# A small FFN with a long convolution in front: K sums straight from the powers, another order ahead of tile 0 and in tiles 1 and 2, and the last tile in two halves

## The chip, the cores and the metric

One NeuronCore of a Trainium2 chip runs the kernel. The metric is the time of one execution on the device in microseconds; three runs of the kernel before gave 215.28, 215.71 and 215.75 us, the median is 215.71.

## What is computed

`x` has 64 sequences, 32 heads and 512 positions. Per head, a kernel K of 512 values is a sum over 64 complex powers, K(h, l) = 2 Re sum_n Cs(h, n) exp(dtA(h, n) l); x, masked by a length per sequence, is convolved with it, and `D` times x is added. On each row of 512 values comes a feed-forward net with quantised operands:

```
beta = mean(|x|);  xq = clip(round(x * sqrt7 / (beta + eps)), -8, 7) * beta
w_eff = clip(round(w / (mean|w| + eps)), -1, 1) * mean|w| * scale      # each of w_gate, w_up, w_down
gate = xq @ w_gate.T;  up = xq @ w_up.T                                # 512 -> 1376
inter = up * square(relu(gate));  inter is rounded to 8 bits by its row's maximum
out = x + inter @ w_down.T                                             # 1376 -> 512
```

## The kernel before, in words

The 2048 rows are worked on in T = 16 tiles of 128 rows (two heads of 64 sequences each). Each engine has its own list of instructions, written out by hand; semaphores join them. What each engine does stands in its own block: SP issues most DMAs, `pool` (GpSimd) some, `pe` is TensorE, `act` ScalarE, `dve` VectorE.

**Ahead of tile 0.** VectorE computes the powers `f` of each head by doubling (`double`, L910) in two tables, 1 to 31 and the multiples of 32, and multiplies the second by `cs`. K is then a sum over the 64 powers, real and imaginary, for each pair (coarse step, fine step): one matmul with 128 rows, 16 columns of weights and 32 moving columns per head. For it VectorE copies the operands of one half of the heads (`g`) to all 128 partitions (`table_b` L936, `table_a` L942). `k_head` (L533) is the matmul; there are 4 heads in part 0, and 12 and 16 in parts 1 and 2 (`K_PARTS` L281). An f32 matmul is two instructions in the trace. `k_copy` (L988) adds D and turns the order, and SP (part 0) and GpSimd's queue (parts 1, 2; L440) store K to DRAM, from where `load_toep` (L328) reads it as a Toeplitz matrix for a tile. SP waits for the store of both last parts before it loads x and the Toeplitz tile of tile 2 (L344, `load_ahead` L347).

Meanwhile each weight matrix is loaded in parts. ScalarE sums its absolute values (`weight_sum` L638); a matmul with a constant takes the mean over the partitions (`mean` L455); VectorE takes the inverse (`weight_mean` L917); `weight_round` rounds to integers (L645 on ScalarE, L955 on VectorE); TensorE turns blocks of it (`turn_inner` L505, groups 0 to 5 for the gate weights, 6 to 11 for the up weights, four PSUM banks in turn), and `weight_copy` clips what was turned, on ScalarE (blocks 2, 4, 5, 9, 11) or VectorE (the others). The down weights are rounded (VectorE L958, ScalarE L649), turned by DMA (`turn_down` L355, on SP) and clipped by `down_copy` (L961) on VectorE. `keep_clock` (L521) is filler: matmuls whose result nobody reads.

**A tile.** `xt` (L467) turns x on TensorE, `xt_copy` on ScalarE takes it out of PSUM, `conv` (L474) is the convolution, `y_mask` (L968, VectorE) masks it, `y_sum` (L662, ScalarE) sums, `y_scale` (L974, VectorE) makes the scales, `y_round` (L667, ScalarE) rounds, `qt` (L486) turns the result and `q_copy` (L983, VectorE) clips it. `products` (L557) are four gate and four up matmuls for each of three blocks of columns (416, 512, 448). `relu_square` (L700) on ScalarE and `gated` (L1040) on VectorE make `inter`. VectorE takes the row's maximum, quantises `inter` to `inter_q` (L1103), SP turns that by DMA (L367), VectorE casts it to `i_t` (L1073), `down` (L594) is the down product of eleven matmuls, and L1121 scales it and adds x; SP stores it (L373). In iteration k TensorE runs the products of tile k, the down product of tile k-1, the q turn of tile k+1 and the convolution of tile k+2; in iteration 1 the down product stands last.

**The last tile.** Its `inter_q` is made in two cuts (L1110) and turned by TensorE instead of DMA (`turn_last` L575, behind eight filler matmuls). ScalarE casts the first six blocks (L719), VectorE the other five (L1080, L1082).

```
            for h in range(HG):
                k_head(2, h)
                if h >= K_EARLY:
                    mm = k_head(1, h)
```

## Time and profile before

| | us |
|---|---|
| median of three runs | 215.71 |
| the profiled execution | 215.85 |
| its span | 214.1 |
| TensorE busy in the span | 180.8 |
| VectorE busy | 168.0 |
| ScalarE busy | 115.0 |

The span is the time from the first to the last event of the profiled execution. A busy time counts the time in which an instruction of the engine ran; matmuls overlap, so that TensorE's is the union. The granted clock is a share of 2.4 GHz: 1.00 is that, 0.50 is 1.2 GHz. In a timeline the brackets say how long the engine was idle before the group, and what released it.

### The profile page before, as it was taken

Reading aid. Unit: us, or ns where it says so; the run is one execution under the profiler, and the core shown is the slowest. Engines: PE = TensorE matmul, PEld = TensorE weight load, DVE = VectorE, ACT = ScalarE, POOL = GpSimd, SP = SyncE. Lnnn points to the kernel's source line nnn. Section 1 sums busy time; section 2 is a strip of 40 time slices with the busy share of each in tenths; the row PEclk is TensorE's granted clock in tenths of the full one; section 3 lists DMA queues with packets and bytes.
Section 4 is the critical chain, followed back from the end, with each engine's and each line's share of the span. In section 5 each row is a group of like instructions: output and inputs, shape, how many; then the busy total and the mean of one; then the engine's idle time right before and its main releaser. Section 6 shows DMA issues by size and latency. Waiting matters only on the chain.

```text
span 214.1 us, 3425 instructions
## 1 busy us (share of the span) xinstructions
PE 180.8 (84%) x1136; PEld 97.0 (45%) x1136; DVE 168.0 (78%) x457; ACT 115.0 (54%) x184; POOL 11.0 (5%) x29
## 2 busy tenths in 40 slices
PE   1011679499969999999999999999999999998882
PEld 1011576345524554545454545454545545454340
DVE  5999886579987979696968787786969696969841
ACT  2277949829943645545463728282736455464410
POOL 4034502000000000000000000000000000000000
PEclk9999999969999999999999999999999999999999
DMA  3999849426999676667483949484757667070722
GB/s 79 370 385 307 283 122 336 140 74 170 168 202 227 189 162 195 146 169 175 139 213 118 221 116 225 114 243 91 227 116 203 126 190 150 15 164 5 165 49 49
DMA packets 43488, 36.61 MB, mean 171 GB/s; under 512 B 29872, under 2 KB 29952, under 8 KB 43472
## 3 DMA queue, kind: packets, MB, share of 16 engines
q1 hardware_dynamic: 42816, 34.93, 62.6%
q10 hardware_dynamic: 336, 1.41, 1.9%
q0 software_dynamic: 320, 0.06, 0.3%
q8 instruction: 9, 0.15, 0.3%
q14 instruction: 7, 0.06, 0.1%
HBM read 25.27 MB, written 4.28 MB: 138 GB/s over the span
## 4 chain that ended last, share of the span: by engine, by line
PE 71%; DVE 11%; ACT 8%; issue 3%; DMA 3%; SPq 2%; DVEq 0%
PE down_ps L607 18%; PE gate_ps L566 16%; PE up_ps L571 15%; PE conv_ps L481 15%; PE tr_act_ps L471 2%; DMA int_gate<-int_down 2%; ACT int_up L642 2%; PE tr_dve_ps L494 1%; ACT int_gate L649 1%; ACT int_down L642 1%; ACT int_up L649 1%; DVE inter L1046 1%; PE tr_dve_ps L536 1%; DMA c_in<-in_L_cond_C_dram 1%; SPq L358 1%
## 5 line engine op out<-in xcount | busy, mean ns | idle before, releaser
L705 ACT ACTIVATE g<-gate_ps,gu_scale 128x416 f32<-128x416 f32 (+2 forms) x48 | 30.5, 636 | 66.5 <-issue 55.6
L1046 DVE SCALAR_TENSOR_TENSOR inter<-up_ps,gu_scale,g 128x416 f32<-128x416 f32 (+2 forms) x48 | 33.1, 690 | 18.3 <-ACT g L708 18.2
L566 PE MATMUL gate_ps<-gate_t,q_t 128*128 128x416 bf16 (+2 forms) x192 | 45.2, 358 | 1.1 <-DVE q_t L985 1.1
L571 PE MATMUL up_ps<-up_t,q_t 128*128 128x416 bf16 (+2 forms) x192 | 45.5, 360 | 0.0
L607 PE MATMUL down_ps<-down_t,i_t 128*128 128x512 bf16 (+1 forms) x176 | 40.7, 380 | 2.2 <-DVE i_t L1073 1.0
L481 PE MATMUL conv_ps<-toep,x_t 128*64 128x512 f32 (+3 forms) x256 | 39.1, 449 | 0.1
L1050 DVE TENSOR_REDUCE imax<-inter 128x1 f32<-128x416 f32 (+2 forms) x48 | 30.3, 631 | 1.6
L708 ACT ACTIVATE g<-g 128x416 f32<-128x416 f32 (+2 forms) x48 | 28.1, 586 | 1.5
L571 PEld LDWEIGHTS up_ps<-up_t,q_t 128*128 128x128 bf16 x192 | 18.8, 98 | 18.5 <-issue 0.2
L607 PEld LDWEIGHTS down_ps<-down_t,i_t 128*128 128x128 bf16 (+1 forms) x176 | 17.0, 98 | 22.4 <-DVE i_t L1073 1.4
L481 PEld LDWEIGHTS conv_ps<-toep,x_t 128*64 128x64 f32 x256 | 17.2, 139 | 20.7 <-issue 16.8
L566 PEld LDWEIGHTS gate_ps<-gate_t,q_t 128*128 128x128 bf16 x192 | 17.6, 98 | 16.1 <-issue 2.2
L971 DVE SCALAR_TENSOR_TENSOR y<-steps,lens,conv_ps 128x512 f32<-128x512 f32 x16 | 12.0, 747 | 5.5 <-PE conv_ps L481 5.3
L1103 DVE TENSOR_SCALAR inter_q<-inter,iscale 128x1376 int16<-128x1376 f32 x15 | 14.0, 937 | 0.5
L1121 DVE SCALAR_TENSOR_TENSOR o_sb<-down_ps,oscale,x_res 128x512 f32<-128x512 f32 x16 | 11.9, 744 | 2.8 <-PE down_ps L607 2.8
L669 ACT ACTIVATE y_r<-y,round_col,yscale 128x512 f32<-128x512 f32 x16 | 12.8, 801 | 0.3 <-DVE yscale L981 0.3
L665 ACT ACTIVATE y_r<-y 128x512 f32<-128x512 f32 x16 | 9.9, 616 | 4.5 <-DVE y L971 4.5
L463 PE MATMUL down_ps<-wsum,averaging 128*128 128x1 f32 x14 | 3.1, 327 | 10.6 <-ACT int_gate L642 10.2
L471 PE MATMUL tr_act_ps<-ident,x_in 128*128 128x128 f32 x64 | 9.9, 278 | 0.0
L471 PEld LDWEIGHTS tr_act_ps<-ident,x_in 128*128 128x128 f32 x64 | 8.1, 146 | 2.9 <-issue 0.2
L660 ACT COPY x_t<-tr_act_ps 128x512 f32<-128x512 f32 x16 | 9.1, 567 | 0.0
L642 ACT ACTIVATE int_gate<-raw_gate 128x3072 bf16<-128x3072 f32 (+1 forms) x2 | 5.1, 2550 | 6.6 <-DMA raw_gate<-in_L_ffn_w_gate_dram 6.6
(170 smaller groups left out, 165.4 us busy)
## 6 DMA issues: line engine op xcount, KB each, us to landing
toep<-k_back SPq DMA_DIRECT2D x16, 512.0 KB, 5.1
x_in<-in_x_dram SPq DMA_DIRECT2D x32, 128.0 KB, 2.8
x_res<-in_x_dram SPq DMA_DIRECT2D x32, 128.0 KB, 4.0
out_dram<-o_sb SPq DMA_DIRECT2D x32, 128.0 KB, 2.5
raw_gate<-in_L_ffn_w_gate_dram SPq DMA_DIRECT2D x1, 1536.0 KB, 7.2
raw_up<-in_L_ffn_w_up_dram SPq DMA_DIRECT2D x1, 1536.0 KB, 13.9
raw_down<-in_L_ffn_w_down_dram ACTq DMA_DIRECT2D x1, 1376.0 KB, 6.9
raw_down<-in_L_ffn_w_down_dram SPq DMA_DIRECT2D x1, 1376.0 KB, 9.0
```

The source lines that it names most:

```text
L471: mm = pe.transpose(tr_act_ps[:, i * P:(i + 1) * P], x_in[p][:, i * P:(i + 1) * P], ident[:])
L481: mm = pe.matmul(conv_ps[half * B:(half + 1) * B, 0:L - i * P], x_t[:, i, half * B:(half + 1) * B], toep[p][:, half, i * P:L], start=(i == ...
L566: mm = pe.matmul(gate_ps[bank][:, 0:cn], q_t[p][:, i, :], gate_t[:, i, c0:c0 + cn], start=(i == 0), stop=(i == KB - 1))
L571: mm = pe.matmul(up_ps[bank][:, 0:cn], q_t[p][:, i, :], up_t[:, i, c0:c0 + cn], start=(i == 0), stop=(i == KB - 1))
L607: mm = pe.matmul(down_ps[:], i_t[0:r, c, :], down_t[0:r, c, :], start=(c == 0), stop=(c == IB - 1))
L669: nc.scalar.activation(y_r[:], y[:], ACT.Identity, bias=round_col[:], scale=yscale[:]).then_inc(y_rounded, 1)
L705: nc.scalar.activation(g2[bank][:, 0:cn], gate_ps[bank][:, 0:cn], ACT.Relu, scale=gu_scale[p][:, 0:1]).then_inc(relu_done, 1)
L708: nc.scalar.activation(g2[bank][:, 0:cn], g2[bank][:, 0:cn], ACT.Square).then_inc(g2_ready, 1)
L971: v.scalar_tensor_tensor(out=y[:], in0=steps[:], scalar=lens[:], in1=conv_ps[:, ::-1], op0=ALU.is_lt, op1=ALU.mult).then_inc(y_masked, 1)
L1046: v.scalar_tensor_tensor(out=inter[:, c0:c0 + cn], in0=up_ps[bank][:, 0:cn], scalar=gu_scale[p][:, 1:2], in1=g2[bank][:, 0:cn], op0=ALU.mu ...
L1050: return v.tensor_reduce(imax[:, c:c + 1], inter[:, c0:c0 + cn], AX.X, ALU.max, apply_absolute_value=True)
L1103: v.tensor_scalar(inter_q[:, 0:I], inter[:], iscale[:], None, ALU.mult).then_inc(inter_quant, 1)
```

## The change

`mean` is one matmul (two instructions) whose columns, one for each part of the sums, VectorE adds up; the mean of the gate weights is read between the products and the sums of the doubling from 4. The K sums take their operands from `f` and from a single table `ka` on the partitions where they stand: for each head two matmuls of 64 rows, real and imaginary, that accumulate. The order of the parts is changed (the second half of the heads comes before the rest of the first), and TensorE's order ahead of tile 0 is: part 0, mean of the up weights, x turn of tile 0, turns 3 to 8, part 1, convolution of tile 0, x turn of tile 1, turns 9 to 11, part 2, q turn. VectorE's and ScalarE's orders follow. The down product of tile 0 moves from the end of iteration 1 into iteration 2, and its output with it; ScalarE rounds y of tile 2 before the last relu and square of tile 1; VectorE copies the second half of the down weights after the quantising of tile 1. Of the last tile, ScalarE quantises the last five blocks and casts them, VectorE the first six; the down product runs as two halves of 256 columns in two PSUM banks, each scaled, added and stored by itself, the last store on two queues; two filler matmuls are left of eight, and the two ahead of tile 0's convolution are gone.

```diff
         f = sb("f", [P, 2, 2 * HG, JB + 1])
-        ka = [sb(f"ka{g}", [P, HG, JA]) for g in range(2)]
-        kb = [sb(f"kb{g}", [P, HG, JB]) for g in range(2)]
+        ka = sb("ka", [P, 2, HG, JA])
...
         K_EARLY = 4
-        K_PARTS = [(0, 0, K_EARLY), (0, K_EARLY, HG), (1, 0, HG)]
+        K_PARTS = [(0, 0, K_EARLY), (1, 0, HG), (0, K_EARLY, HG)]
+        LAST = [(conv_ps, slice(0, L // 2)), (up_ps[0], slice(L // 2, L))]
...
                     turn_down(0)
-                if k >= 2:
+                if k == T + 1:
+                    sp.wait_ge(out_ready, T)
+                    for half in range(2):
+                        sp.dma_start(in_dram(out, T - 1, half)[:, LAST[0][1]],
+                                     o_sb[p][half_rows(half), LAST[0][1]]).then_inc(stored[p], 16)
+                    sp.wait_ge(out_ready, T + 1)
+                    sp.dma_start(in_dram(out, T - 1, 0)[:, LAST[1][1]],
+                                 o_sb[p][half_rows(0), LAST[1][1]]).then_inc(stored[p], 16)
+                elif k >= 2:
...
                 n = len(ARRIVE[m]) - 1
-                for i in range(n):
-                    mm = pe.matmul(down_ps[:, m:m + 1], averaging[:], wsum[:, m, i:i + 1],
-                                   start=(i == 0), stop=(i == n - 1))
+                mm = pe.matmul(down_ps[:, 4 * m:4 * m + n], averaging[:], wsum[:, m, 0:n], start=True, stop=True)
...
-            def k_head(i, h):
-                g = K_PARTS[i][0]
-                dst = tr_dve_ps[32 * i:32 * i + JA, h * JB:(h + 1) * JB]
-                return pe.matmul(dst, ka[g][:, h], kb[g][:, h], start=True, stop=True)
-            for h in range(K_EARLY):
-                mm = k_head(0, h)
-            mm.then_inc(k_summed, 1)
+            def k_sums(i):
+                g, h0, h1 = K_PARTS[i]
+                rows_g = slice(g * N, (g + 1) * N)
+                for h in range(h0, h1):
+                    for c in range(2):
+                        mm = pe.matmul(tr_dve_ps[32 * i:32 * i + JA, h * JB:(h + 1) * JB], ka[rows_g, c, h],
+                                       f[rows_g, c, h, 0:JB], start=(c == 0), stop=(c == 1))
+                mm.then_inc(k_summed, 1)
+            k_sums(0)
             mean(1)
-            pe.wait_ge(tables_ready, 2)
-            for h in range(HG):
-                k_head(2, h)
-                if h >= K_EARLY:
-                    mm = k_head(1, h)
-            mm.then_inc(k_summed, 1)
+            xt(0, 0, 0)
             turn_inner(0, 0, range(3, IG))
-            xt(0, 0, 0)
             turn_inner(1, IG, range(0, 3))
-            keep_clock(2)
+            k_sums(1)
...
             turn_inner(1, IG, range(3, IG))
+            k_sums(2)
...
             def turn_last():
                 pe.wait_ge(y_masked, T)
-                keep_clock(8)
+                keep_clock(2)
...
             def down(m, k):
                 if k == T:
-                    pe.wait_ge(it_act_copied, 1)
-                else:
-                    pe.wait_ge(it_dve_copied, m)
+                    pe.wait_ge(it_dve_copied, T)
+                    for bank, cols in LAST:
+                        for c in range(IB):
+                            if c == IT_SPLIT:
+                                pe.wait_ge(it_act_copied, 1)
+                            r = P if c < IB - 1 else IR
+                            mm = pe.matmul(bank[:, 0:L // 2], i_t[0:r, c, :], down_t[0:r, c, cols],
+                                           start=(c == 0), stop=(c == IB - 1))
+                        mm.then_inc(down_done, 1)
+                    return
+                pe.wait_ge(it_dve_copied, m)
...
                 for c in range(IB):
-                    if c == IT_SPLIT and k == T:
-                        pe.wait_ge(it_dve_copied, m)
...
                     products(m, p, 1, k)
+                    if k == 2:
+                        down(1, 1)
...
                     conv(m + 2, j + 1, p)
-                if k == 1:
-                    down(m, k)
...
             weight_copy(2)
+            xt_copy(0)
...
             weight_copy(5)
-            xt_copy(0)
...
                 if k == T:
-                    act.wait_ge(it_turned, 1)
+                    act.wait_ge(iscale_ready, 1)
+                    act.wait_ge(it_loaded, 16 * (T - 1))
+                    cut = slice(IT_SPLIT * P, I)
+                    nc.scalar.activation(inter_q[:, cut], inter[:, cut], ACT.Copy,
+                                         scale=iscale[:]).then_inc(inter_quant, 1)
+                    act.wait_ge(it_turned, 2)
                     act.wait_ge(down_done, T - 1)
-                    nc.scalar.copy(i_t[:, 0:IT_SPLIT, :].rearrange("p c t -> p (c t)"),
-                                   tr_act_ps[:, 0:IT_SPLIT * P // 2].bitcast(I16)).then_inc(it_act_copied, 1)
+                    nb = IB - 1 - IT_SPLIT
+                    nc.scalar.copy(i_t[:, IT_SPLIT:IB - 1, :].rearrange("p c t -> p (c t)"),
+                                   tr_dve_ps[:, 0:nb * P // 2].bitcast(I16))
+                    nc.scalar.copy(i_t[0:IR, IB - 1, :], tr_dve_ps[0:IR, nb * P // 2:(nb + 1) * P // 2].bitcast(I16)
+                                   ).then_inc(it_act_copied, 1)
+                    act.wait_ge(out_ready, T + 1)
+                    act.dma_start(in_dram(out, T - 1, 1)[:, LAST[1][1]],
+                                  o_sb[1][half_rows(1), LAST[1][1]]).then_inc(stored[1], 16)
...
                     y_round(1)
+                if k == 1:
+                    y_round(2)
...
                     relu_square(2)
-                if 1 <= k < T - 1:
+                if 2 <= k < T - 1:
...
-            def double(k, n, heads):
+            def double(k, n, heads, between=None):
...
                              [f[:, c:c + 1, 0:heads, k:k + 1] for c in range(2)])
+                if between:
+                    between()
...
             def weight_mean(m, step):
                 dve.wait_ge(w_mean_ps, m + 1)
-                v.tensor_copy(wscale[:, m:m + 1], down_ps[:, m:m + 1])
-                step(v.tensor_scalar(weps[:, m:m + 1], down_ps[:, m:m + 1], EPS, None, ALU.add))
+                step(v.tensor_reduce(wscale[:, m:m + 1], down_ps[:, 4 * m:4 * m + len(ARRIVE[m]) - 1], AX.X, ALU.add))
+                step(v.tensor_scalar(weps[:, m:m + 1], wscale[:, m:m + 1], EPS, None, ALU.add))
...
             while k < JB:
-                double(k, k, 2 * HG if k < JA else HG)
+                double(k, k, 2 * HG if k < JA else HG, (lambda: weight_mean(0, step)) if k == 4 else None)
                 k *= 2
-                if k == 8:
-                    weight_mean(0, step)
...
             def k_copy(i):
                 g, h0, h1 = K_PARTS[i]
-                dve.wait_ge(k_summed, min(i, 1) + 1)
+                dve.wait_ge(k_summed, i + 1)
...
-            table_b(0)
-            table_a(0)
-            table_b(1)
+            v.tensor_tensor(ka[:, 0, :, ::-1], by_csr[:, 0], by_csi[:, 1], ALU.subtract)
+            v.scalar_tensor_tensor(out=ka[:, 1, :, ::-1], in0=by_csi[:, 0], scalar=-1.0, in1=by_csr[:, 1],
+                                   op0=ALU.mult, op1=ALU.subtract).then_inc(tables_ready, 1)
+            weight_copy(0)
...
             k_copy(0)
+            weight_copy(1)
             weight_mean(1, step)
-            table_a(1)
-            weight_copy(0)
-            weight_copy(1)
...
             weight_copy(7)
-            k_copy(1)
-            k_copy(2)
+            weight_copy(8)
...
             step(v.tensor_tensor(wscale[:, 0:2], wscale[:, 0:2], scl[:, 0:2], ALU.mult))
-            weight_copy(8)
+            k_copy(1)
             y_mask(0)
+            weight_copy(10)
             y_scale(0, 0, step)
-            weight_copy(10)
+            k_copy(2)
...
+                def add_out(n, bank, cols, done):
+                    q = n % 2
+                    dve.wait_ge(down_done, done)
+                    dve.wait_ge(res_loaded[q], 32 * (n // 2 + 1))
+                    wait(dve, stored[q], 32 * (n // 2))
+                    v.scalar_tensor_tensor(out=o_sb[q][:, cols], in0=bank[:, 0:cols.stop - cols.start],
+                                           scalar=oscale[q][:], in1=x_res[q][:, cols],
+                                           op0=ALU.mult, op1=ALU.add).then_inc(out_ready, 1)
...
                     down_copy(1)
-                if k == 1 or k == T - 1:
+                if k == 2:
+                    y_scale(3, 1, step)
+                if k in (1, 2, T - 1):
                     gated(1)
+                if k == 2:
+                    add_out(0, down_ps, slice(0, L), 1)
...
                     v.tensor_copy(i_t[:], it_int[:]).then_inc(it_dve_copied, 1)
-                if 2 <= k < T - 1:
+                if 3 <= k < T - 1:
...
                 if k == T:
-                    dve.wait_ge(it_turned, 2)
+                    dve.wait_ge(it_turned, 1)
                     dve.wait_ge(down_done, T - 1)
...
+                    v.tensor_copy(i_t[:, 0:IT_SPLIT, :].rearrange("p c t -> p (c t)"),
+                                  tr_act_ps[:, 0:IT_SPLIT * P // 2].bitcast(I16)).then_inc(it_dve_copied, 1)
+                    add_out(T - 2, down_ps, slice(0, L), T - 1)
+                    for h, (bank, cols) in enumerate(LAST):
+                        add_out(T - 1, bank, cols, T + h)
-                if k < T - 1 and k != 1:
+                    v.tensor_copy(i_t[:, 0:IT_SPLIT, :].rearrange("p c t -> p (c t)"),
+                                  tr_act_ps[:, 0:IT_SPLIT * P // 2].bitcast(I16)).then_inc(it_dve_copied, 1)
+                    add_out(T - 2, down_ps, slice(0, L), T - 1)
+                    for h, (bank, cols) in enumerate(LAST):
+                        add_out(T - 1, bank, cols, T + h)
+                if k < T - 1 and k not in (1, 2):
...
                     step(gated(2))
-                if k == 1:
-                    down_copy(0)
...
                     step(v.tensor_scalar(gam127[:], gamma[:], EPS, 1.0 / 127.0, ALU.add, ALU.mult))
-                    step(v.reciprocal(iscale[:], gam127[:]))
                     if k != T - 1:
+                        step(v.reciprocal(iscale[:], gam127[:]))
...
+                        v.reciprocal(iscale[:], gam127[:]).then_inc(iscale_ready, 1)
+                        dve.wait_ge(iscale_ready, 1)
                         dve.wait_ge(it_loaded, 16 * (T - 1))
-                        for cut, ready in ((slice(0, IT_SPLIT * P), last_quant), (slice(IT_SPLIT * P, I), inter_quant)):
-                            v.tensor_scalar(inter_q[:, cut], inter[:, cut], iscale[:], None,
-                                            ALU.mult).then_inc(ready, 1)
+                        cut = slice(0, IT_SPLIT * P)
+                        v.tensor_scalar(inter_q[:, cut], inter[:, cut], iscale[:], None,
+                                        ALU.mult).then_inc(last_quant, 1)
                 if k == 1:
+                    down_copy(0)
                     y_mask(3)
-                if k is None or k >= 1:
...
+                if 2 <= k < T - 1:
+                    add_out(m - 1, down_ps, slice(0, L), m)
```

## Rows read from the trace of the kernel before

**Rows 1.** Page, section 1: busy time and share of the span of each engine.

```profile
PE 180.8 (84%) x1136; PEld 97.0 (45%) x1136; DVE 168.0 (78%) x457; ACT 115.0 (54%) x184; POOL 11.0 (5%) x29
```

**Rows 2.** Chain that ended last, start us, us, work: first gate products of two tiles.

```profile
97.17 0.81 PE gate_ps L566 x4
...
107.27 0.81 PE gate_ps L566 x4
```

**Rows 3.** Timeline (start us, us, engine, line, operation): the mean and rounding of gate weights.

```profile
15.11 1.01 PE L463 MATMUL down_ps<-wsum,averaging 128*128 128x1 f32 x4 [10.24 <-ACT int_gate L642]
...
16.14 0.44 DVE L907 TENSOR_TENSOR inter<-f 128x256 f32<-128x256 f32 x1
...
17.60 2.86 ACT L649 ACTIVATE int_gate<-raw_gate,winv 128x3072 int16<-128x3072 f32 x1 [2.55 <-DVE winv L922]
```

**Rows 4.** Timeline, 24 to 38 us: K sums, turns, first copy behind them, convolution.

```profile
24.83 0.60 PE L536 MATMUL tr_dve_ps<-kb,ka 128*16 128x32 f32 x8 [1.51 <-DVE ka L946]
...
28.60 1.89 PE L536 MATMUL tr_dve_ps<-kb,ka 128*16 128x32 f32 x56 [1.40 <-DVE ka L946]
...
31.25 1.38 PE L517 MATMUL up_ps<-ident_bf,int_gate 128*128 128x128 bf16 x12
...
32.35 1.41 ACT L656 ACTIVATE gate_t<-up_ps 128x1024 bf16<-128x1024 int16 x2 [3.41 <-PE up_ps L517]
...
33.11 1.06 PE L517 MATMUL gate_ps<-ident_bf,int_up 128*128 128x128 bf16 x16
...
34.98 2.37 PE L481 MATMUL conv_ps<-toep,x_t 128*64 128x512 f32 x16
```

**Rows 5.** Timeline, 41 to 48 us: tile 0's start and tile 1's convolution.

```profile
41.30 0.40 PE L494 MATMUL tr_act_ps<-ident_bf,y_r 128*128 128x128 bf16 x4 [2.30 <-ACT y_r L669]
...
42.08 3.01 DVE L1024 TENSOR_REDUCE wsum<-raw_down 128x1 f32<-128x2752 f32 x1
...
42.22 0.88 PE L566 MATMUL gate_ps<-gate_t,q_t 128*128 128x416 bf16 x4 [0.52 <-DVE q_t L985]
...
44.25 3.50 PE L481 MATMUL conv_ps<-toep,x_t 128*64 128x512 f32 x16
...
47.80 0.75 DVE L971 SCALAR_TENSOR_TENSOR y<-steps,lens,conv_ps 128x512 f32<-128x512 f32 x1 [1.53 <-PE conv_ps L481]
```

**Rows 6.** Window of that convolution: us, TensorE busy, granted clock, DMA share, GB/s.

```profile
44.20:47.80 3.60, 3.60 (x18) 0.67 0.04 13
```

**Rows 7.** Timeline, 61 to 67 us, TensorE at the end of tile 1.

```profile
61.04 0.40 PE L494 MATMUL tr_dve_ps<-ident_bf,y_r 128*128 128x128 bf16 x4 [1.28 <-ACT y_r L669]
61.50 2.37 PE L481 MATMUL conv_ps<-toep,x_t 128*64 128x512 f32 x16
64.45 2.54 PE L607 MATMUL down_ps<-down_t,i_t 128*128 128x512 bf16 x11 [0.58 <-DVE down_t L966]
```

**Rows 8.** Timeline, from 204 us: filler matmuls, cast, last down product, output, stores.

```profile
204.20 1.89 PE L525 MATMUL conv_ps<-steps,ident_bf 128*128 128x512 bf16 x8
...
206.47 0.80 ACT L719 CAST i_t<-tr_act_ps 128x768 bf16<-128x768 int16 x1 [5.13 <-PE tr_act_ps L582]
...
207.32 2.55 PE L607 MATMUL down_ps<-down_t,i_t 128*128 128x512 bf16 x11 [0.61 <-ACT i_t L719]
209.91 0.75 DVE L1121 SCALAR_TENSOR_TENSOR o_sb<-down_ps,oscale,x_res 128x512 f32<-128x512 f32 x1 [2.61 <-PE down_ps L607]
...
210.69 1.11 SPq L373 DMA_DIRECT2D out_dram<-o_sb  x2
```

**Rows 9.** DMA issues: KB each, median us from issue to landing.

```profile
toep<-k_back SPq DMA_DIRECT2D x16, 512.0 KB, 5.1
...
k_back<-k_sb POOLq DMA_DIRECT2D x1, 24.0 KB, 2.9
```

**Rows 10.** Groups by shape, K sums: busy us, mean ns of one.

```profile
L536 PE MATMUL tr_dve_ps<-kb,ka 128*16 128x32 f32 x64 | 2.5, 240 | 2.9 <-DVE ka L946 2.9
...
L536 PEld LDWEIGHTS tr_dve_ps<-kb,ka 128*16 128x16 f32 x64 | 2.2, 121 | 3.3 <-DVE ka L946 3.3
```

24 lines of the change are left out of this document (2 added, 22 removed).

## The prediction

> **What bounds the kernel now.** I read the busy shares first [rows 1]: TensorE is busy for 84% of the span, VectorE for 78%, ScalarE for 54%. That average mixes three stages, so I then read the chain of work that ended last, in order of time. From 66.8 us to about 195 us it is TensorE alone: each tile's first gate product starts 10.10 us after the last one's [rows 2] and nothing waits. The change leaves these tiles alone, so what it can win lies ahead of tile 3 and behind tile 15, and whatever TensorE gains before tile 3 is carried unchanged to the tail. The rest I read from timelines, engine by engine.
>
> Ahead of tile 0 the chain goes: sums of the weights on ScalarE, the mean on TensorE and VectorE, the rounding on ScalarE, the K sums and the turns on TensorE, then ScalarE's queue (two weight copies, the x copy, a rounding and a sum over weights, the sum of y), which had waited 3.41 us for the turns behind the K sums [rows 4]. Behind it, tile 0's products start at 42.22, and the convolution of tile 1 takes 3.50 us where that of tile 0 took 2.37 [rows 4, 5]; the granted clock of that stretch is 0.67 [rows 6]. In tile 1 TensorE waits 1.28 us before the q turn and 0.58 us before the down product [rows 7]. At the end it is one serial chain: quantise, turn, cast, down product, scale and add, store [rows 8].
>
> **The sum is made against the profiled execution**: 215.85 us, with a span of 214.1; the 1.75 us around the span I leave as they are. It is 0.14 us over the median of the runs shown, which I take off at the end.
>
> **Part 1, the means.** The mean of the gate weights was four instructions in 1.01 us and becomes two, some 0.5 us (15.11 to 15.6). VectorE now reads it between the products and the sums of a doubling, that is behind the product that ends at 16.14 + 0.44 = 16.58 [rows 3]. Three dependent steps of about 0.2 us give the inverse at 17.2; the rounding on ScalarE then starts at 17.23 where it was 17.60: 0.37 us earlier. ScalarE's queue is unbroken from there to the rounding of the rest of the gate weights, which ends at 27.66 (28.03 before). The mean of the up weights, six such instructions, becomes two as well, 0.5 us; its result comes at about 25.7 and no longer ends a wait.
>
> **Part 2, tables and K sums.** Four copies of 0.42 us on VectorE go, and the table of both halves is two operations of the same 0.42 us each, on 128 partitions where it was 64 (I take the same time, since the number of elements per partition is the same). The first K sums can start at 24.05 instead of 24.83. The price: 64 matmul instructions become 128. Before, the run of 56 took 1.89 us, 30 ns apart behind a latency of 0.24; the first 8 took 0.60 us, 51 ns apart [rows 4]. No 64-row matmul is in the trace. With half the rows it might take half, 15 ns: the low bound (on the path it would give back 64 x 15 ns = 1.0 us). 51 ns is the high one, and I take 30, since 56 instructions are the better sample and the number of columns stays. So: 0.8 us for the first part, 2.1 for the second (64), 1.6 for the third (48). The first part, its copy and its store on SP all come 0.7 us earlier, and with them the loads of the first two Toeplitz tiles.
>
> **Part 3, the order ahead of tile 0.** TensorE: the x turn runs in the idle time before 27.7. Then 20 turns from 27.7 and 24 more. Here is a clock effect: the turns from 31.25 run about 0.107 us apart (12 in 1.38 less a latency of some 0.2), those from 33.11 about 0.056 apart (16 in 1.06) [rows 4], so by these durations TensorE went from 1.2 to 2.4 GHz near 32.5, after 4 us of unbroken work (the granted clock is written as 1.00 on both sides). I put the rise at about 32. The turns then end at 32.2, the second K sums at 34.2, and the convolution of tile 0 starts there instead of at 34.98 (the two filler matmuls are gone; its Toeplitz tile was issued at 28.71 and is now issued at 28.0, which with the page's 5.1 us is 33.1). It ends at 36.55, and VectorE masks y at 36.6. ScalarE is no longer late: copies to 31.0, rounding to 33.4, sum to 35.9, so it waits for y and sums it by 38.1. But weight copy 10 now stands ahead of the scale of y on VectorE, and it waits for a turn behind the convolution: it runs from 37.9 to 38.6. The scale is ready at 39.25, y rounded at 40.1, q turned at 40.55 (the third K sums end at 39.9 and are just covered), q copied at 41.0 behind the K copy, and the products start at 41.07. Against 42.22 that is 1.15 us.
>
> **Part 4, the clock.** Before, TensorE had idled 2.30 us before the q turn, and 0.52 us after it [rows 5], and the clock then fell to 1.2 GHz. Now the K sums fill that hole and 0.3 and 0.5 us remain. I take it that the clock holds: tile 0's first products take 1.57 us instead of 2.03 and the convolution 2.37 instead of 3.50, together 1.6 us. The next link is VectorE: its sum over the down weights (3.01 us) and the first gated block (some 1.25 us) end at 45.15, and only then can it mask y of tile 1, where it was 47.80 [rows 5]. So 2.65 of 2.75 us are kept.
>
> **Part 5, what was moved behind.** The third K copy ends at 40.55 where it was 36.35; its store on GpSimd's queue lands 2.9 us after its issue [rows 9], and SP's loads of x and the Toeplitz tile for tile 2 stand behind it: x issued at 43.4, the tile at 44.6, landed by 47 and, with 5.1 us, by 49.7. TensorE wants them at 47.2 and 49.5. I count nothing for this, since the queues are nearly empty by then, with 0.7 us as the high bound.
>
> **Part 6, the first down product.** It moves from behind tile 1 into tile 2, behind the second products. The wait of 0.58 us before it (it waited for the copy of the transposed down weights, [rows 7]) goes. The 1.28 us before the q turn stays in another form: the convolution of tile 3 needs the x copy on ScalarE, which is behind the same work whether the rounding of y comes before or after the last relu and square. VectorE's order in tile 2 becomes down copy, mask, block 0, scale, block 1, output of tile 0, cast of tile 1: in the new times the cast ends at 68.1 and TensorE wants it at 68.7. So 0.5 us of cover; I take a loss of 0.1. Products of tile 3: 2.65 + 0.58 - 0.1 = 3.1 us earlier. In tile 2 SP's next x and Toeplitz loads stand behind the later output of tile 0 (67.75 against 67.78), which is some 4 us ahead of their use.
>
> **Part 7, the tail** (in the old times). Six of eight filler matmuls go (1.89 us for eight, less a latency of 0.17): 6 x 0.215 = 1.3 us, so the first turns end at 205.2 instead of 206.45; the second turns wait for ScalarE's share of the quantising (608 columns at 0.86 ns, from the rounding of 3072 in 2.86, [rows 3]: 0.75 us from 203.75), done by 204.5, and end at 205.5. VectorE casts six blocks in about 0.6 us, and the down product starts at 205.83 against 207.32. Its halves of 256 columns take 11 x 0.11 each and end at 207.2 and 208.4; ScalarE's casts are done at 206.35, just ahead of the sixth block. The output of tile 14 lies between, covered. The last half is scaled and added in 0.5 us (0.75 for 512 columns, [rows 8]), ready at 208.95 instead of 210.66. The last stores are issued from two queues, at 209.0, where the second of the pair was issued at 211.2. Gain 2.2 us; 1.5 if the small stores or casts cost as much as the large, 2.7 if the waits vanish.
>
> **Sum:** 215.85 - 3.1 - 2.2 = 210.55, less 0.14: **210.4 us**.
>
> **The rivals.**
> The clock falls again, 0.17. For it: the new work in the hole is turns and 32-column matmuls, and two short holes stay. Against it: just such work, K sums and turns from 28.60 to 32.4, raised the clock [rows 4]. It costs up to 1.6 us: **212.0**.
>
> The Trainium skill, "TensorE: Matmul & The Clock Gate", Part 4 on the transpose mode, says that transposes don't count as busy for the clock; by that rule this rival would be the likely one, but the rise at 32 us in this trace speaks against it.
>
> K sums at 51 ns, 0.12. The second part costs 1.3 us more and delays the convolution; the third costs 1.0 more and is no longer covered before the q turn. The start of tile 0 is then 43.2, the clock holds: **212.5**.
>
> The ends ahead of tile 0 don't move, 0.07: weight copy 10, the third K copy and late loads eat what the order gave, and the clock falls. Then only 0.5 and 2.2 us are left: **213.0**.
>
> Slower, 0.05. Weight load and matmul of the 64-row form are not overlapped. A load takes 121 ns and a matmul 240 ns by itself [rows 10]; at 121 ns each, the 112 instructions of the last two parts cost 112 x 0.09 = 10.2 us more, some **220.6**. It turns slower from 80 ns each (5.3 / 112 = 47 ns over my 30). Against it: 128-row K sums, with the same 16 columns loaded, ran 30 ns apart. The Trainium skill, "TensorEngine Tiling (Array Packing)", Key Properties, says that a change of the tiling mode drains TensorE. Here the mode would change twice for each part, six times in all, and not for each matmul; no row shows such a drain.
>
> The forecast itself has 0.59.
>
> **How the numbers follow.** The likeliest is the forecast, 210.4. Its own range is 209.2 to 211.5: 0.5 and 0.7 us for the tail, 0.7 for the prologue's end and the loads. The range of 8 in 10 takes in the two rivals at 212.0 and 212.5: 209.0 to 212.7. A measurement of this kernel can tell about 0.2% (0.4 us) from no change. All cases but the slower one lie over 2 us below 215.71. Of the 0.07 of the fourth case I give 0.02 to the same time, should the tail's gain not come either. That leaves 0.93 for faster, 0.02 for the same, 0.05 for slower.
>
> **What would show it.** Right: the q turn of tile 0 with under 0.6 us of idle time before it, the convolution of tile 1 in 2.4 us at a granted clock of 1.00, K sums of 64 instructions in about 2.1 us, no wait before the first down product, a last down product in two groups, begun 6.1 us before the end of the span. Wrong: K sums over 3 us, a clock of 0.5 in the first tile, TensorE waiting for x or the Toeplitz tile of tile 2, or for a cast in tile 2.

## The result, and the profile after

The changed kernel took 212.11 us in the median of four runs (211.16 to 212.98), the kernel before 215.5 (213.64 to 215.75); the ratio is 0.986, with a 95% interval of 0.982 to 0.990. The profiled execution took 211.90 us, with a span of 210.0, against 215.85 and 214.1: 3.95 us less. The forecast was 210.4. The direction was right, and the time lies in the range of 8 in 10 (209.0 to 212.7), but above the forecast's own range (209.2 to 211.5); in the profiled execution the gain is 1.35 us smaller than forecast.

One thing of the runs has to be known. The kernel before doesn't take one time: of 43 runs, 20 took 215.2 to 215.9 us (the long runs) and 23 took 213.4 to 214.6. All those seen ahead of the prediction were of the first group. What makes the difference is not shown; what the traces say of it stands with the experiments on the tail and on the hole.

The page of the changed kernel: busy shares, and the granted clock in tenths (9 is 0.9 or more), in 40 slices of 5.25 us.

```profile
PE 178.1 (85%) x1179; PEld 98.2 (47%) x1195; DVE 165.4 (79%) x450; ACT 115.8 (55%) x186; POOL 10.6 (5%) x29
...
PEclk9999958999999999999999999999999999999999
```

The busy share hardly moved [rows 1]; the clock dips in the sixth and seventh slice, 26 to 37 us, and nowhere else; the steady tiles still follow each other every 10.10 us. The gain is at both ends. TensorE ahead of tile 0, and below it VectorE's mask, weight copy 10 and mask of tile 1, in the timeline of the changed kernel; [rows 3 to 5] are the same places before:

```profile
23.75 0.64 PE L546 MATMUL tr_dve_ps<-f,ka 64*16 64x32 f32 x16 [1.06 <-DVE ka L1008]
...
28.28 1.38 PE L525 MATMUL up_ps<-ident_bf,int_gate 128*128 128x128 bf16 x12
...
32.15 2.47 PE L546 MATMUL tr_dve_ps<-f,ka 64*16 64x32 f32 x64
34.54 2.38 PE L489 MATMUL conv_ps<-toep,x_t 128*64 128x512 f32 x16
...
38.50 1.58 PE L546 MATMUL tr_dve_ps<-f,ka 64*16 64x32 f32 x48
40.67 0.40 PE L502 MATMUL tr_act_ps<-ident_bf,y_r 128*128 128x128 bf16 x4 [0.59 <-ACT y_r L680]
41.59 0.88 PE L571 MATMUL gate_ps<-gate_t,q_t 128*128 128x416 bf16 x4 [0.52 <-DVE q_t L995]
...
43.10 2.37 PE L489 MATMUL conv_ps<-toep,x_t 128*64 128x512 f32 x16
...
36.97 0.75 DVE L981 SCALAR_TENSOR_TENSOR y<-steps,lens,conv_ps 128x512 f32<-128x512 f32 x1 [1.56 <-PE conv_ps L489]
38.43 0.69 DVE L963 TENSOR_SCALAR up_t<-gate_ps 128x1024 bf16<-128x1024 int16 x1 [0.72 <-PE gate_ps L525]
...
45.68 0.74 DVE L981 SCALAR_TENSOR_TENSOR y<-steps,lens,conv_ps 128x512 f32<-128x512 f32 x1
```

The x turn and all 44 turns that stood behind the K sums [rows 4] now come before the middle ones; the convolution of tile 0 starts 0.44 us earlier than in [rows 4], the first products 0.63 us, and the convolution of tile 1 takes 2.37 us where it took 3.50 [rows 5]. The windows of the changed kernel (us, TensorE busy, granted clock, DMA share, GB/s):

```profile
28.00:30.00 2.00, 2.00 (x23) 0.50 0.35 115
...
32.00:34.00 2.00, 2.00 (x52) 0.72 1.02 271
...
41.00:48.00 7.00, 6.40 (x41) 1.00 0.51 151
```

At tile 1's convolution the clock is 1.00, where it was 0.67 [rows 6]. But the turns from 28 to 32 us run at 0.50, which is 1.2 GHz: 12 turns in 1.38 us, as in [rows 4]. (There the record said 1.00 beside turns of the same duration; the durations decide.) The rise comes between 32 and 34 us, inside the middle K sums. Tile 2 waited for neither x nor its Toeplitz tile: its convolution started at 49.98, behind a q turn that had waited 0.17 us for ScalarE.

Tiles 1 and 2: TensorE, then VectorE's cast, then SP's issues.

```profile
64.58 2.54 PE L618 MATMUL down_ps<-down_t,i_t 128*128 128x512 bf16 x11
...
69.59 2.55 PE L618 MATMUL down_ps<-down_t,i_t 128*128 128x512 bf16 x11 [0.52 <-DVE i_t L1096]
...
74.61 0.88 PE L571 MATMUL gate_ps<-gate_t,q_t 128*128 128x416 bf16 x4
...
69.01 0.53 DVE L1096 CAST i_t<-it_int 128x1408 bf16<-128x1408 int16 x1 [0.93 <-DMA it_int<-inter_q]
...
61.08 0.59 SPq L333 DMA_DIRECT2D toep<-k_back  x1
...
62.94 1.49 SPq L369 DMA_TRANSPOSE it_int<-inter_q  x1
```

The wait of 0.58 us before the first down product [rows 7] is gone, but the second one in iteration 2 waited 0.52 us for the cast, and the cast 0.93 us for SP's DMA turn: issued at 62.94, landed at 68.99, 6.05 us later, behind the Toeplitz load of 512 KB issued at 61.08. A wait for a cast in tile 2 was one of the signs that the prediction had named for being wrong.

The tail, which answers [rows 8]:

```profile
203.48 1.38 PE L608 MATMUL conv_ps<-down_t,i_t 128*128 128x256 bf16 x11 [0.37 <-DVE i_t L1102]
...
204.10 1.92 SPq L383 DMA_DIRECT2D out_dram<-o_sb  x2
...
206.06 1.23 SPq L375 DMA_DIRECT2D out_dram<-o_sb  x2
206.10 0.48 DVE L1068 SCALAR_TENSOR_TENSOR o_sb<-up_ps,oscale,x_res 128x256 f32<-128x256 f32 x1 [0.72 <-PE up_ps L608]
206.61 0.56 ACTq L741 DMA_DIRECT2D out_dram<-o_sb  x1
207.34 0.74 SPq L378 DMA_DIRECT2D out_dram<-o_sb  x1
```

From the first products of tile 3 to the end of the span it is 135.4 us, where it was 137.2: 1.8 us less.

### The profile page after: what moved, and what is told of

It reads as the page before. It is cut to its first block, busy times and chain, and to the rows that moved or that the text cites. A ratio compares the mean times of both kernels' runs of the same rounds, so it can differ in the third digit from the quotient of the medians.

```text
span 210.0 us, 3525 instructions
## 1 busy us (share of the span) xinstructions
PE 178.1 (85%) x1179; PEld 98.2 (47%) x1195; DVE 165.4 (79%) x450; ACT 115.8 (55%) x186; POOL 10.6 (5%) x29
## 4 chain that ended last, share of the span: by engine, by line
PE 64%; DMA 3%; DVE 2%; issue 1%; ACT 1%; SPq 1%; DVEq 0%
PE down_ps L618 16%; PE gate_ps L571 14%; PE conv_ps L489 14%; PE up_ps L576 14%; DMA it_int<-inter_q 3%; PE tr_act_ps L479 2%; PE tr_dve_ps L502 1%; PE conv_ps L608 1%; PE up_ps L608 1%; SPq L388 1%; DVE i_t L1096 1%; DVE inter L1055 0%; ACT g L716 0%; ACT g L719 0%; DVE i_t L1102 0%
## 5 line engine op out<-in xcount | busy, mean ns | idle before, releaser
L716 ACT ACTIVATE g<-gate_ps,gu_scale 128x416 f32<-128x416 f32 (+2 forms) x48 | 30.5, 636 | 66.0 <-issue 53.3
L576 PE MATMUL up_ps<-up_t,q_t 128*128 128x512 bf16 (+2 forms) x191 | 44.8, 357 | 0.1
L571 PE MATMUL gate_ps<-gate_t,q_t 128*128 128x448 bf16 (+2 forms) x178 | 42.3, 356 | 1.9 <-DVE q_t L995 1.1
L618 PE MATMUL down_ps<-down_t,i_t 128*128 128x512 bf16 (+1 forms) x164 | 37.9, 380 | 1.7 <-DVE i_t L1096 1.7
L489 PE MATMUL conv_ps<-toep,x_t 128*64 128x512 f32 (+3 forms) x256 | 38.0, 439 | 1.2 <-ACT x_t L671 1.2
L618 PEld LDWEIGHTS down_ps<-down_t,i_t 128*128 128x128 bf16 (+1 forms) x165 | 16.0, 98 | 20.7 <-DVE i_t L1096 2.4
L1068 DVE SCALAR_TENSOR_TENSOR o_sb<-down_ps,oscale,x_res 128x512 f32<-128x512 f32 x15 | 11.1, 743 | 0.0
L472 PE MATMUL down_ps<-wsum,averaging 128*128 128x2 f32 (+1 forms) x6 | 1.4, 296 | 11.3 <-ACT int_gate L653 10.5
```

Source lines behind the costliest of these rows:

```text
L489: mm = pe.matmul(conv_ps[half * B:(half + 1) * B, 0:L - i * P], x_t[:, i, half * B:(half + 1) * B], toep[p][:, half, i * P:L], start=(i == ...
L571: mm = pe.matmul(gate_ps[bank][:, 0:cn], q_t[p][:, i, :], gate_t[:, i, c0:c0 + cn], start=(i == 0), stop=(i == KB - 1))
L576: mm = pe.matmul(up_ps[bank][:, 0:cn], q_t[p][:, i, :], up_t[:, i, c0:c0 + cn], start=(i == 0), stop=(i == KB - 1))
L618: mm = pe.matmul(down_ps[:], i_t[0:r, c, :], down_t[0:r, c, :], start=(c == 0), stop=(c == IB - 1))
L716: nc.scalar.activation(g2[bank][:, 0:cn], gate_ps[bank][:, 0:cn], ACT.Relu, scale=gu_scale[p][:, 0:1]).then_inc(relu_done, 1)
```

## The experiments

All times are medians. The kernel before ran beside each group of kernels: 214.49 us (17 runs) beside the first four, 214.18 (11) beside the next four, 215.22 (11) beside the last three. Since its share of long runs differs from group to group (8 of 17, 3 of 11, 6 of 11), I compare kernels within a group and by their traces. A trace has a clean measure of its own: three points, the start of tile 0's products (41.59 in the changed kernel, 42.22 before), the start of tile 3's (74.61; 76.91), and from there to the end (135.4; 137.2).

**The tail alone.** The kernel before with the edits of the last tile (abridged):

```diff
-                keep_clock(8)
+                keep_clock(2)
...
+                    for bank, cols in LAST:
+                        for c in range(IB):
...
+                    act.wait_ge(out_ready, T + 1)
+                    act.dma_start(in_dram(out, T - 1, 1)[:, LAST[1][1]],
```

> The kernel before with the last-tile part alone (halves, shared quantising and casts, two fillers, stores). Theory: the parts add up, and the tail holds 1.8 us of the change's gain: 213.9 us against 215.7, the last down product starts 1.5 us earlier measured from the one before it, and the order ahead of tile 3 is as before. Rival (the prologue made nearly all of the gain, the tail's serial chain only moved its wait to the stores): under 0.8 us of gain, 215.0.

Measured 213.1 us, 0.9905 of the kernel before (0.987 to 0.994): a gain of 1.4 us in the medians, though five of its six runs lay at 212.8 to 213.3, some 2.5 us under the long runs of the kernel before. In its trace the last down product starts 3.97 us after the one before it, where it was 5.51: 1.54 us less, as expected. It is 134.7 us from tile 3 to the end, 2.5 less than before, so the tail is worth more alone than it was in the changed kernel's trace. Its stores say why:

```profile
205.16 1.13 SPq L384 DMA_DIRECT2D out_dram<-o_sb  x2
...
207.15 0.48 DVE L1087 SCALAR_TENSOR_TENSOR o_sb<-up_ps,oscale,x_res 128x256 f32<-128x256 f32 x1 [0.72 <-PE up_ps L614]
207.66 0.55 SPq L379 DMA_DIRECT2D out_dram<-o_sb  x1
```

SP issued the pair of tile 14 in 1.13 us; in the changed kernel the same pair took 1.92, and held up the stores of the first half, and these the last one, which started at 207.34 although its data were ready at 206.58. The rival (under 0.8) falls: the tail is a part of the gain by itself.

The same trace tells something of the kernel before, whose order ahead of tile 3 it has unchanged:

```profile
41.13 1.57 PE L577 MATMUL gate_ps<-gate_t,q_t 128*128 128x416 bf16 x4 [0.52 <-DVE q_t L1013]
44.02 2.53 PE L492 MATMUL conv_ps<-toep,x_t 128*64 128x512 f32 x16
```

Behind a hole of 2.64 us ahead of the q turn the granted clock is 0.50 from 41 to 44 us. From tile 0's first products (41.13) to the mean of the down weights behind the convolution of tile 1 (46.48) it is 5.35 us, against 5.46 in the trace before (42.22 to 47.68): the fall of the clock costs about the same here. Yet tile 0 starts 1.09 us earlier than before, and that comes from stretches further ahead: the mean of the up weights took 0.83 us and not 1.44, the K sums started at 27.84 and not 28.60, and the 12 turns that had taken 1.38 us [rows 4] took 0.91. So this execution was 3.7 us shorter than the profiled one before, of which only 2.5 are the tail.

**Without the move of the first down product.** The changed kernel with

```diff
-                    if k == 2:
-                        down(1, 1)
...
+                if k == 1:
+                    down(m, k)
```

and the orders of VectorE and ScalarE that belong to it.

> The changed kernel with the first down product, the output of tile 0, the rounding of y and the copy of the down weights back where they were. Theory: the move gives nothing, because the wait it took away (0.6 us before the down product at the end of tile 1) came back as a wait for the DMA that turns the quantised block of tile 1; same time as the changed kernel within 0.2 us, products of tile 3 at 74.5 us in the trace. Rival (prediction as written): the move is worth 0.5 us, products of tile 3 at 75.1 and 0.5 us slower than the changed kernel.

Measured 212.03 us, 0.9868 of the kernel before (0.983 to 0.991), which can't be told from the changed kernel. The trace tells more:

```profile
62.49 2.54 PE L618 MATMUL down_ps<-down_t,i_t 128*128 128x512 bf16 x11 [0.90 <-DVE down_t L974]
...
74.95 0.88 PE L571 MATMUL gate_ps<-gate_t,q_t 128*128 128x416 bf16 x4
```

From tile 0's products (41.51) to tile 3's it is 33.44 us, in the changed kernel 33.02. The move is worth 0.42 us in this pair of traces, near the 0.5 of the prediction (two more traces with the same instructions in this stretch have 32.85 and 33.11); my theory after the result, that it gives nothing, falls. The wait for the down weights is 0.90 us here, not 0.58 [rows 7]: TensorE was ready for them 2.3 us earlier than before, but VectorE could start their last copy, which waits for a DMA turn, only 1.96 us earlier. The move takes these 0.90 away and pays back 0.52.

**The hole in front of tile 0, filled.** The kernel before with

```diff
             turn_inner(1, IG, range(3, IG))
+            for _ in range(10):
+                pe.matmul(down_ps[:], ident_bf[:], steps[:, 0:L // 2].bitcast(BF16), start=True, stop=True)
             qt(0)
```

> The kernel before with ten filler matmuls of 512 columns (2.2 us) into an unused bank in the 2.3 us in which TensorE waited for the rounded y of tile 0. Nothing else is changed. Theory: the hole made the clock fall; with it filled the convolution of tile 1 takes 2.37 us, not 3.50, VectorE masks y of tile 1 at 46.3 and not 47.8, and the time falls by 1.5 us to 214.2. Rival (the fall is not tied to the hole, or VectorE is the next bound anyway): the granted clock still reads 0.5 at 43 to 46.6 us, or the time stays at 215.7.

Measured 214.09 us, 0.997 of the kernel before (0.995 to 1.000); 12 runs, all between 213.91 and 214.70, none in the group above 215.2 to which 8 of the 17 runs of the kernel before beside it belong.

```profile
41.06 0.40 PE L494 MATMUL tr_act_ps<-ident_bf,y_r 128*128 128x128 bf16 x4 [0.48 <-ACT y_r L671]
...
43.49 2.37 PE L481 MATMUL conv_ps<-toep,x_t 128*64 128x512 f32 x16
```

The idle time before the q turn is 0.48 us instead of 2.30, the convolution takes 2.37 us instead of 3.50, at a granted clock of 1.00. From tile 0's first products to the mean of the down weights it is 3.82 us (41.98 to 45.80), where it was 5.46, and 5.35 in the trace of the tail alone. So the hole is what lets the clock fall, and the fall costs some 1.5 us.

But the median fell by 0.4 us only, since more than half of the runs of the kernel before were short without the filler. It would be easy to say that the clock held in those; it is not shown, and the trace of the tail alone speaks against it, since there the clock fell and the front was short all the same. The mean granted clock of each run separates the groups and doesn't settle it: it was 0.989 to 0.991 in the 17 long runs beside the experiments, and in the 22 others 0.981 to 0.983 (15) or 0.996 to 0.999 (7), while the tail's trace, in which the clock was at 0.50 from 27.8 to 30.5 us and again from 41 to 44, has 0.984. No trace of the kernel before in a short run exists.

**K sums of 128 rows in the new order.** The changed kernel with the two tables and the matmul of the K sums back, and VectorE's four copies:

```diff
-                    for c in range(2):
-                        mm = pe.matmul(tr_dve_ps[32 * i:32 * i + JA, h * JB:(h + 1) * JB], ka[rows_g, c, h],
-                                       f[rows_g, c, h, 0:JB], start=(c == 0), stop=(c == 1))
+                    mm = pe.matmul(tr_dve_ps[32 * i:32 * i + JA, h * JB:(h + 1) * JB], ka[g][:, h], kb[g][:, h],
+                                   start=True, stop=True)
```

> The changed kernel with the K sums as 128-row matmuls again (half the instructions, four copies of 0.42 us on VectorE back), in the new order of parts. Theory: the 64-row form costs its instructions (64 in 2.47 us against 32 in some 1.2), so the middle part is 1.2 us shorter, but the first table is ready 0.85 us later, and the second table's 1.7 us on VectorE hold up weight copy 3; the first products start within 0.5 us of the changed kernel's 41.6, either way. Rival (64-row matmuls were the saving): first products later by over 0.7 us. Second rival (the doubled instructions were a net loss): first products over 0.7 us earlier.

Measured 212.8 us, 0.987 of the kernel before (0.983 to 0.992); four runs at 212.8 to 213.2 and two at 210.7 and 211.0. TensorE, then the window of tile 0's start:

```profile
33.17 1.89 PE L545 MATMUL tr_dve_ps<-kb,ka 128*16 128x32 f32 x32
...
39.09 0.87 PE L545 MATMUL tr_dve_ps<-kb,ka 128*16 128x32 f32 x24
41.26 0.40 PE L503 MATMUL tr_act_ps<-ident_bf,y_r 128*128 128x128 bf16 x4 [1.29 <-ACT y_r L680]
42.17 1.57 PE L571 MATMUL gate_ps<-gate_t,q_t 128*128 128x416 bf16 x4 [0.52 <-DVE q_t L995]
...
41.00:48.00 7.00, 6.22 (x31) 0.76 0.47 143
```

The first products start at 42.17, 0.58 us after the changed kernel's: outside the 0.5 of my theory by little, short of the 0.7 of the first rival; the second rival falls. In these two traces the price of one instruction goes with the clock. The 128-row form takes 53 ns behind turns that run at the lower level (32 in 1.89 us less a latency of 0.2) and 28 at the higher (24 in 0.87). The 64-row form does the same. Two windows of 0.2 us inside the middle part of the changed kernel (the number in brackets counts the instructions in flight, each of which lasts 0.24 us, so that many start within 0.44 us):

```profile
32.40:32.60 0.20, 0.20 (x8) 0.50 1.01 215
33.40:33.60 0.20, 0.20 (x13) 1.00 1.05 340
```

That is 55 ns at a granted clock of 0.50 and 34 at 1.00; 64 in 2.05 us without the lower level are 29. So in these stretches the number of rows doesn't matter and the number of instructions does, and 51 ns, the prediction's high bound, is near the price at the lower level (the last section has a stretch that doesn't fit). In this kernel the turns were held up for 0.77 us at 30.6, the clock rose only behind the middle K sums, and the 32 instructions took 1.89 us where 64 took 2.47 in the changed kernel. Between turns and q turn fewer instructions leave a hole of 1.29 us, and the clock falls: products in 1.57 us, a granted clock of 0.76 in the window. In the changed kernel, where a hole of 0.59 us is left, the 48 instructions of the third part were also filler.

**The changed kernel again**, beside the next three.

> The changed kernel unchanged, beside the three that follow. Theory: its runs spread over 1.5 us because TensorE's clock rises at different moments ahead of tile 0; median 212.0, the granted clock not at 0.5 between 41 and 48 us in the trace.

Measured 212.34 us (210.96 to 213.45), 0.990 of the kernel before (0.985 to 0.994). Its trace has tile 0 at 41.36, tile 3 at 74.21, a wait of 0.37 us before the second down product, and 135.6 us from tile 3 to the end: SP's pair of stores took 2.27 us. The granted clock from 41 to 48 us is 1.00, as expected. The clock ahead of tile 0 did take another course: the first 16 K sum instructions took 1.03 us and not 0.64, and the middle ones 2.05 and not 2.47. Of the ten runs of the changed kernel in both timings, the four whose mean granted clock was 1.00 took 210.96 to 211.94 us, the six below it 211.90 to 213.45; that fits the theory on the spread, but one more trace doesn't prove it.

**The scale of y ahead of weight copy 10.**

```diff
-            weight_copy(10)
             y_scale(0, 0, step)
+            weight_copy(10)
```

> The changed kernel with the scale of y of tile 0 ahead of weight copy 10 on VectorE, as before the change. Theory: copy 10 stands on the path (it waited 0.72 us for a turn, and the scale behind it was ready 0.6 us after the sum of y); now the scale comes at 38.5 us and y is rounded at 39.3, and the third K sums (to 40.1) are next late: q turn 0.3 to 0.6 us earlier, 0.4 us faster than the changed kernel. Rival (the third K sums and the K copy on VectorE bound it already): no gain.

Measured 211.41 us, 0.9848 of the kernel before (0.981 to 0.989), 0.9 under the changed kernel beside it.

```profile
39.60 0.40 PE L502 MATMUL tr_act_ps<-ident_bf,y_r 128*128 128x128 bf16 x4
40.65 0.88 PE L571 MATMUL gate_ps<-gate_t,q_t 128*128 128x416 bf16 x4 [0.65 <-DVE q_t L995]
```

The q turn starts at 39.60, behind the third K sums without a wait, 0.84 us earlier than in the changed kernel beside it (40.44); 0.3 of this is that its K sums started earlier (32.02 against 32.34). So 0.5 us at the q turn are the order's, within the 0.3 to 0.6 expected. The products start 0.71 us earlier, of which 0.4 are the order's: the q copy now stands behind the K copy on VectorE.

**The Toeplitz load of tile 4 behind the DMA turn.**

```diff
-                    load_ahead(m + 3, 1 - p)
+                    load_ahead(m + 3, 1 - p, k != 1)
...
+                if k == 2:
+                    sp.wait_ge(conv_done, 3)
+                    load_toep(4, 0)
```

> The changed kernel with the Toeplitz load of tile 4 issued on SP behind the DMA that turns the quantised block of tile 1, not ahead of it. Theory: the turn landed 6 us after its issue because the load of 512 KB was ahead of it in the DMA engines; now it lands in about 4 us, VectorE's cast no longer waits 0.93 us and TensorE's second down product in iteration 2 starts 0.5 us earlier; products of tile 3 0.5 to 0.7 us earlier. Rival (the DMA turn is slow by itself there): it still lands after 6 us.

Measured 211.37 us, 0.9854 of the kernel before (0.982 to 0.989), 1.0 under the changed kernel beside it.

```profile
68.67 2.54 PE L622 MATMUL down_ps<-down_t,i_t 128*128 128x512 bf16 x11
...
62.25 1.55 SPq L370 DMA_TRANSPOSE it_int<-inter_q  x1
63.84 0.80 SPq L333 DMA_DIRECT2D toep<-k_back  x1
```

The turn, issued at 62.25, landed in 4.2 us instead of 6.0, the down product starts without a wait, and tile 3 comes at 73.67 against 74.21 with the same start of tile 0 (41.34 and 41.36): 0.5 us, as expected. The turn was also issued 0.6 us earlier. The other traces agree in the main: with the load ahead and this place in the new order it took 5.7 to 6.1 us in four more and 5.3 in one (the early filler below), with the load behind 5.0 and 4.8 in the two below. So the load ahead of it was the cause of the wait.

**The last stores on two queues.** ScalarE's queue takes one half of each store of the tiles 14 and 15.

```diff
+                    act.wait_ge(out_ready, T - 1)
+                    act.dma_start(in_dram(out, T - 2, 1), o_sb[0][half_rows(1), :]).then_inc(stored[0], 16)
```

> The changed kernel with the stores of the last two tiles split by halves over the queues of SP and ScalarE (before: SP issued five of six in a row). Theory: SP's issues, 0.5 to 1.4 us each, were the last link: the last one started at 207.34 although its data were ready at 206.6; now both start at 206.6, and the time falls by 0.7 us. Rival (the landing of the stores, not the issue, is the end): under 0.2 us.

Measured 211.12 us, 0.984 of the kernel before (0.980 to 0.988), 1.2 under the changed kernel beside it, the whole set of runs within 0.8 us.

```profile
203.93 0.49 SPq L380 DMA_DIRECT2D out_dram<-o_sb  x1
203.94 0.54 ACTq L738 DMA_DIRECT2D out_dram<-o_sb  x1
...
205.23 1.67 SPq L375 DMA_DIRECT2D out_dram<-o_sb  x2
205.24 1.70 ACTq L741 DMA_DIRECT2D out_dram<-o_sb  x2
205.92 0.48 DVE L1068 SCALAR_TENSOR_TENSOR o_sb<-up_ps,oscale,x_res 128x256 f32<-128x256 f32 x1 [0.72 <-PE up_ps L605]
```

Each queue issues three stores and both last ones follow their data at once. From tile 3 to the end it is 134.7 us, against 135.6 in the changed kernel beside it: 0.9 us, the tail's full 2.5 us against the kernel before.

**The three together**: the edits of the last three sections.

> The changed kernel with the three edits that follow from its trace: scale of y of tile 0 ahead of weight copy 10, Toeplitz load of tile 4 behind the DMA turn of tile 1's block, last stores shared by two queues. Theory: each took away a wait at another place of the one chain, so the gains add: 0.7 + 0.5 + 0.8 = 2.0 us under the changed kernel, 210.0 us. Rival (they share cover; VectorE's order in iteration 2 takes back what the earlier start gives): 210.8.

Measured 209.52 us, 0.976 of the kernel before (0.972 to 0.981), 0.5 us under my sum, and the rival (210.8) falls. In the trace the wait before the q turn and that before the down product are gone. Against the first trace of the changed kernel tile 0 comes 0.3 us earlier (41.27), the way from there to tile 3 is 0.7 us shorter (32.33) and the rest 0.7 (134.7): the gains add, to 1.7 us there. The changed kernel itself was not timed beside this one, so the larger difference of the medians (2.6 to 2.8) is less sure.

**Filler in the early holes.** The changed kernel with filler matmuls behind the first turns and behind the x turn of tile 0.

```diff
             turn_inner(0, 0, range(3))
+            keep_clock(2)
...
             xt(0, 0, 0)
+            keep_clock(3)
             turn_inner(0, 0, range(3, IG))
```

> The changed kernel with five filler matmuls of 512 columns in the two holes of TensorE before the turns of the gate weights (two behind the first turns, three behind the x turn of tile 0). Theory: the turns from 27.5 to 32.1 us ran 107 ns apart, at the lower level, because TensorE had idled before; with the holes filled the clock is up before 30 us, the 44 turns take under 3.6 us instead of 4.7 and the middle K sums start at 31 us or earlier, the time falls by 0.7 us, and the spread of the runs shrinks. Rival (ScalarE's copies and roundings pace the turns): the turns run 56 ns apart but start as late, and under 0.3 us is gained.

Measured 209.62 us, 0.977 of the kernel before (0.972 to 0.982), a spread of 208.4 to 210.8: more of a gain than I expected, and the spread didn't shrink.

```profile
29.56 1.84 PE L525 MATMUL gate_ps<-ident_bf,int_up 128*128 128x128 bf16 x16
31.24 0.61 PE L525 MATMUL up_ps<-ident_bf,int_up 128*128 128x128 bf16 x8
```

In its trace the clock was not up before 30 us: the 16 turns from 29.56 still took 1.84 us. The middle K sums then took 2.05 us instead of 2.47 and tile 0 started at 40.80, 0.8 us earlier. The other 1.4 us by which this trace is under that of the changed kernel are not the filler's: the DMA turn landed in time, and SP's pair of stores took 1.13 us.

**All four**: the three and this filler.

> All four edits of the two kernels beside this one. Theory: 209.4 us if the filler's gain adds to the three. Rival (ScalarE's queue up to the sum over the down weights is the next bound once the turns are faster, or the filler delays the K sums): same as the three edits alone, 210.0.

Measured 208.67 us (208.37 to 209.95), 0.974 of the kernel before (0.969 to 0.978), where I expected 209.4; the rival (210.0) falls. It is the fastest of all, some 3.4 us under the changed kernel, which was not timed beside it.

```profile
29.16 1.06 PE L526 MATMUL gate_ps<-ident_bf,int_up 128*128 128x128 bf16 x16
...
30.90 2.05 PE L548 MATMUL tr_dve_ps<-f,ka 64*16 64x32 f32 x64
...
39.79 0.88 PE L574 MATMUL gate_ps<-gate_t,q_t 128*128 128x416 bf16 x4 [0.78 <-DVE q_t L1001]
```

In this run the clock was up by 29 us (16 turns in 1.06), the K sums follow at 30.90 and tile 0 starts at 39.79. So the filler can do what it was meant to do, but not in each run.

## Why the prediction was right, and where its sizes were off

Of the 1.35 us that are missing, 0.8 lie ahead of tile 3 (products 2.3 us earlier, not 3.1), 0.4 in the tail, and the rest outside the span. The median of 212.11 lies next to the 212.0 of the first rival; that is chance as far as the trace shows, for in the profiled execution the clock held.

**Means and tables.** The rounding on ScalarE started at 16.96 (forecast 17.23), the first K sums at 23.75 (24.05); VectorE was 0.25 us earlier from the start in this execution. The turns ended at 32.15 (32.2).

**K sums.** The middle part took 2.47 us where I had 2.1, since its first 0.9 us ran at the lower level, at a price (55 ns) near my high bound of 51. The rate of 30 ns was right for the higher level. The convolution of tile 0 so came at 34.54 (34.2).

**The way to tile 0.** The gain was 0.63 us, not 1.15. The chain was the one I had described, and two terms of it were mis-sized: 0.34 of the 0.52 us come from the middle K sums, which made the convolution late, and the rest from weight copy 10, which I had put on the path from 37.9 to 38.6 and which ran from 38.43 to 39.12, since it waits for turns behind that convolution. From there on every step came 0.5 us late. The third K sums and the K copy were covered, as forecast. The experiment with the scale first shows that copy 10 cost 0.5 us at the q turn and 0.4 at the products: I had seen the price and not said that the order alone could save it.

**The clock.** It held, as forecast, and the convolution of tile 1 took 2.37 us. The mask of tile 1 came at 45.68 (45.15), 2.12 us earlier than before. That the filled hole is worth some 1.5 us is shown by the traces with and without it. What failed is what I set against it: I took 215.71 us for the time of the kernel before, and 23 of its 43 runs were 1.1 to 2.3 us under it. This is why the gain in the medians (3.4, and 1.8 beside the changed kernel's second timing) is below that of the two traces. Whether the fall of the clock was missing in those runs, or the early stretch was faster as in the trace of the tail alone, stays open.

Turns and K sums filled the hole, and the clock stayed at 1.00 from 41 to 48 us. That was the rival's place. The Trainium skill, "TensorE: Matmul & The Clock Gate", Part 4, says that transposes don't count as busy for the clock in the way that other matmuls do; by that rule alone the rival would have come; with K sums behind the turns it didn't, and no run here had turns alone in that place. In the trace with early filler, though, the granted clock rose from 0.50 to 1.00 at 31.2 us, when TensorE had run nothing but turns since 27.65.

**The move.** Forecast 0.48, measured 0.42 by the trace without it. The mechanism named for the loss was another: I looked at VectorE's order, which was in time (output of tile 0 done at 68.08), and the prediction has no term for the DMA turn that the cast waits for. It was issued behind x and Toeplitz loads and took 6.05 us, where it took 4.2 in the kernel before. The loss was 0.52 us, where I had put 0.1; that the sum still fits is partly luck, since the wait taken away had grown to 0.90.

**The tail.** Forecast 2.2, measured 1.8 in this trace, and 2.5 where SP's issues didn't get in the way. Casts, halves and fillers were right to 0.1 us: the last down product 3.84 us earlier than in [rows 8], of which 2.3 came from ahead; the last output 1.77 earlier by itself (forecast 1.71). The term that was mis-sized is the end: I had the last stores issued at 209.0, as soon as their data were ready, and left out that SP could still be at the stores before them; here the last one went out 0.76 us behind its data.

None of the four rivals occurred in the profiled execution of the changed kernel: the clock did not fall again, the K sums took 2.47 us and not the 3.4 of the second rival, tile 0 did start earlier, and the kernel was not slower than before.

## What to carry to other kernels

When a wait is removed, ask which transfers now stand close together: the two losses here (a DMA turn behind a 512 KB load, a store behind the issue of another store) were both in the queue of SP, and a different order or a second queue gave them back. Before a saving is read from one trace, look at the spread of the runs: here the kernel before had runs 2 us apart, and the gain in the medians came to between 1.8 and 3.4 us. And before a spread is put down to the one effect in view, look for a trace that has the same instructions in a shorter run. Work that must be done anyway can be the filler for a hole that costs the clock, as the third K sums were here.

## What the runs showed of the hardware that I had not expected

An f32 matmul instruction with 16 columns of weights took 53 to 55 ns in stretches at the lower level of the clock and 28 or 29 (34 in a short window) at the higher, with 64 rows as with 128. One stretch doesn't fit: behind 1.40 us of idle time, 56 of them came in 1.89 us, 30 ns apart, although the turns right after them ran at the lower level [rows 4]; in the trace of the tail alone they did the same while the granted clock read 0.50 from 27.8 to 30.5 us. I can't say why. The first 16 of the changed kernel took 0.64 us in three traces, 1.03 in four without filler and one with it, and 0.82 in the other with filler; where they took 0.64, the x turn behind them took 0.63 us, and 1.09 where they took 1.03, so that TensorE ran at either level there from one execution to the next. Two stores of 128 KB took SP 1.13 us to issue in some traces and 1.65 to 2.27 in others, with the same data and the same order. The granted clock of the record can read 1.00 in a stretch whose matmuls take twice as long as later ones (12 turns in 1.38 us from 31.25, 16 in 1.06 from 33.11 [rows 4]; the record has 1.00 for both); there I went by the durations.
